# Selective scan: three quarters of x by row gathers on GpSimd, coefficients by row scatters

## The reference, cut to what matters

```
x = x + _L0_attn_a_ref(_layernorm(x, axis=-1), W_in, conv_w, conv_b, W_xproj, A_log, D_param, W_out)
x = x + _L0_ffn_ref(...)      # a mixture of 15 experts and a shared one
x = x + _L0_attn_b_ref(...)   # linear attention
...                           # experts, retention, experts, softmax attention, experts
```

## Time and profile before

| | us |
|---|---|
| median of 3 runs (lowest, highest) | 2271.25 (2269.46, 2271.72) |
| the profiled execution, its own time | 2265.08 |
| its span, first to last instruction | 2263.4 |
| busy: TensorE / VectorE / ACT / GpSimd | 1980.8 / 1702.2 / 1016.5 / 498.3 |
| mean granted clock of TensorE | 0.929 |

### The profile page before, as it was taken

One profiled execution on the slowest core, in us unless ns is written; L12 is line 12 of the kernel. 1 busy time (PEld: TensorE's weight loads), 2 busy tenths in 40 slices (PEclk: granted clock), 3 DMA queues, 4 the chain that ended last, 5 costly groups with the idle time before them and its releaser, 6 DMA issues. The chain is left out here.

```text
span 2263.4 us, 35922 instructions
## 1 busy us (share of the span) xinstructions
PE 1980.8 (88%) x12434; PEld 1484.5 (66%) x12434; DVE 1702.2 (75%) x5243; ACT 1016.5 (45%) x1596; POOL 498.3 (22%) x560
## 2 busy tenths in 40 slices
PE   5786799987999867754699978999999999979999
PEld 3554699976999823322699965566556555549998
DVE  6997788865888769999588876766766766628887
ACT  3442244433444333322344444566665665554443
POOL 1110100012000023221100014534533544230000
PEclk8998899998999987776799989999999999989999
DMA  3000100000000000000000000000000000000000
GB/s 97 6 5 4 54 1 1 1 1 1 1 1 2 13 27 1 0 1 0 1 1 1 1 1 1 1 1 1 1 1 1 1 1 1 1 1 6 11 11 15
DMA packets 17638, 15.75 MB, mean 7 GB/s; under 512 B 4209, under 2 KB 16177, under 8 KB 16946
## 3 DMA queue, kind: packets, MB, share of 16 engines
q1 hardware_dynamic: 15152, 12.66, 1.8%
q10 hardware_dynamic: 2306, 0.78, 0.2%
HBM read 10.55 MB, written 2.88 MB: 6 GB/s over the span
## 5 line engine op out<-in xcount | busy, mean ns | idle before, releaser
L2256 DVE TENSOR_REDUCE soft_mx<-psum 128x1 f32<-128x512 f32 (+3 forms) x608 | 380.4, 659 | 198.5 <-PE psum L2127 111.9
L2173 ACT ACTIVATE soft_prob<-psum 128x1024 f32<-128x1024 f32 (+3 forms) x384 | 305.1, 813 | 209.8 <-PE psum L2054 208.9
L2123 PE MATMUL psum<-soft_own,soft_stack 128*128 128x512 f32 (+3 forms) x768 | 250.4, 376 | 18.9 <-DVE soft_mx L2256 16.5
L2054 PE MATMUL psum<-soft_stack,soft_own 128*128 128x512 f32 (+3 forms) x768 | 228.4, 381 | 2.9 <-POOL soft_stack L2029 2.2
L2054 PEld LDWEIGHTS psum<-soft_stack,soft_own 128*128 128x128 f32 x768 | 121.2, 189 | 134.1 <-issue 74.7
L2123 PEld LDWEIGHTS psum<-soft_own,soft_stack 128*128 128x128 f32 x768 | 139.2, 191 | 77.7 <-DVE soft_mx L2256 63.1
L2071 PE MATMUL psum<-soft_prob,soft_v_pad 128*32 128x512 f32 (+3 forms) x1536 | 163.9, 498 | 3.5 <-ACT soft_prob L2173 2.1
L1056 DVE SCALAR_TENSOR_TENSOR x<-psum,ffn1b_cw,x 128x128 f32<-128x128 f32 x512 | 144.0, 343 | 30.1 <-PE psum L934 21.3
L1056 DVE SCALAR_TENSOR_TENSOR x<-psum,ffn0b_cw,x 128x128 f32<-128x128 f32 x512 | 144.1, 343 | 29.9 <-PE psum L934 21.5
L1056 DVE SCALAR_TENSOR_TENSOR x<-psum,ffn1a_cw,x 128x128 f32<-128x128 f32 x512 | 144.1, 344 | 29.8 <-PE psum L934 21.0
L1056 DVE SCALAR_TENSOR_TENSOR x<-psum,ffn0a_cw,x 128x128 f32<-128x128 f32 x512 | 144.1, 344 | 29.5 <-PE psum L934 21.0
(11 more groups left out here) (435 smaller groups left out, 3845.4 us busy)
## 6 DMA issues: line engine op xcount, KB each, us to landing
s_ffn_w<-in_ffn_w SPq DMA_DIRECT2D x4, 1024.0 KB, 8.3
out_x<-x SPq DMA_DIRECT2D x8, 256.0 KB, 2.3
x<-in_x SPq DMA_DIRECT2D x4, 384.0 KB, 7.4
mamba_coef_dram<-mamba_out_coef SPq DMA_DIRECT2D x8, 96.0 KB, 1.6
s_ret_w<-in_ret_w SPq DMA_DIRECT2D x1, 640.0 KB, 3.5
x<-in_x SPq DMA_DIRECT2D x4, 128.0 KB, 3.9
s_ret_cos<-in_ret_cos SPq DMA_DIRECT2D x1, 512.0 KB, 4.9
s_ret_sin<-in_ret_sin SPq DMA_DIRECT2D x1, 512.0 KB, 5.5
```

The costliest lines, as they stand in the source:

```text
L2054: ins = pe.matmul(e_ps[:, n % 2, j, low(n):BLK], own[:, u % 3, 2 * pair + j, kt * P:(kt + 1) * P], stack[:, u % HT, qb * BLK + low(n):(qb ...
L2123: ins = pe.matmul(per_head[:, n, :], stack[:, u % HT, i * P:(i + 1) * P], own[:, u % 3, g, half * BLK:half * BLK + width], start=(n == 0), ...
L2173: nc.scalar.activation(prob[:, done % PROBS, :, low(n):BLK], e_ps[:, n % 2, :, low(n):BLK], ACT.Exp, scale=float(HD) ** -0.5).then_inc(exp ...
L2256: nc.vector.tensor_reduce(mx[:, i, half, heads.start:heads.stop], bank[:, 0:width * len(heads)].rearrange("p (g k) -> p g k", k=width), AX ...
```

## The change

Three quarters of x (token tiles 2 to 7 of each batch row) are no longer loaded by four DMAs of SP, but by 24 indirect DMAs of GpSimd, 128 rows each, the row numbers taken from a new constant table `rows` of 128 x 32 integers (column n holds the rows of tile n). The table is one more load in `weights_rest`. GpSimd issues the gathers behind its first two `invert`s and a wait for `weights_rest`, ahead of its first tile. The stores of `out_coef` go from SP to GpSimd as indirect DMAs that scatter 128 rows with a column of the same table; GpSimd instead of SP waits at the end for all eight.

```
@@ shape_constants
+            "rows": np.arange(TILES * P, dtype=np.int32).reshape(TILES, P).T,
@@ mamba_scan, block.sync
-            for copies, loaded in (x_first, x_rest, later):
+            for copies, loaded in (x_first, later):
                 for dst, src in copies:
                     sp.dma_start(dst, src).then_inc(loaded, 16)
-            for tt in range(TPB):
-                sp.wait_ge(out_coef_ready, tt + 1)
-                sp.dma_start(coef_dram[slice(tt * P, (tt + 1) * P), :], out_coef[:, :, :, :]).then_inc(coef_stored, 16)
-            sp.wait_ge(coef_stored, 16 * TPB)
@@ block.gpsimd, scan
                 nc.gpsimd.tensor_copy(out_coef[:, 2, :, :], cc[:, :, 0:NS]).then_inc(out_coef_ready, 1)
+                pool.wait_ge(out_coef_ready, tt + 1)
+                pool.indirect_dma_start(coef_dram[:, :], bass.IndirectOffsetOnAxis(const["rows"][:, tt:tt + 1], 0),
+                                        out_coef[:, :, :, :].rearrange("p k b s -> p (k b s)"), None)\
+                    .then_inc(coef_stored, 16)
                 if more == 2:
                     norm.invert(pool, tt + 2)
@@ block.gpsimd
             norm.invert(pool, 0)
             norm.invert(pool, 1)
+            pool.wait_ge(*all_of(*weights_rest))
+            dst, src, loaded = x_rest
+            for a in range(2, TPB):
+                for b in range(BATCH):
+                    n = b * TPB + a
+                    pool.indirect_dma_start(dst[:, n, :], None, src,
+                                            bass.IndirectOffsetOnAxis(const["rows"][:, n:n + 1], 0))\
+                        .then_inc(loaded, 16)
             tiles(scan)
+            pool.wait_ge(coef_stored, 16 * TPB)
@@ block.vector
-            dve.wait_ge(*all_of(*x_rest))
+            dve.wait_ge(x_rest[2], 16 * BATCH * (TPB - 2))
@@ hybrid_kernel
-        x_rest = [(homes[:, b, 2:TPB, :], tokens[:, b, 2:TPB, :]) for b in range(BATCH)]
+        x_rest = x, arrays["x"].rearrange("b t c -> (b t) c")
-        loads = ((x_first, load_x_first), (x_rest, load_x_rest), (weights_first, load_first),
+        loads = ((x_first, load_x_first), (*x_rest, load_x_rest), (weights_first, load_first),
```

## The result

The median went from 2271.36 us (four runs; the first three of them gave the 2271.25 above) to 2291.75 us (four runs, 2290.36 to 2293.00): ratio 1.0093, 95% interval 1.0081 to 1.0105, which is 20.4 us slower. The forecast was 2294. The profiled execution took 2290.36 us, 25.3 more than the one of before.

A forecast was written before the change was run, and what follows sets the result against it. VectorE paces the scan; its wait for x before the first tile decides. 14.6 + 29.8 + 3.0 + 2.2 = 49.6 us against 28.60 gives 21.0, plus 2.0 for the clock: 23.0 us, median 2294 us, range 2279 to 2315.

The forecast's parts named there:

- scatters hidden: In each tile, a 1.24 us scatter on GpSimd fits its idle time: counted 0, 4.6 us kept for the range.
- Price of a gather: On GpSimd ahead of the first tile: 1.24 us per gather, 29.8 us for 24, bounds 7.9 and 52.8.
- Start: Gathers begin once `weights_rest` has landed: 10.6 + 4.0 = 14.6 us, not before 13.22, at the latest 20.4.
- Stalls by VectorE: VectorE's convolutions and SiLU product hold up GpSimd's gathers in the head: 3 us, bounds 0 and 5.9.
- Landing: The last gather lands 2.2 us after it is issued, bounds 1.6 and 5.2.
- Clock: TensorE's longer pause starts the first tile at the low clock: 2.0 us on VectorE's path, bounds 0 and 4.
- Tiles behind: From VectorE's first step inputs to the stage's end: distance unchanged but for about 2 us.
- Hidden: Rival: gathers done by 28.60 us, at most 0.52 us each, time stays at 2271 us; chance 0.09.
- half hidden: Rival: gathers on GpSimd cost 0.52 to 0.9 us each; at 0.75 us, time 2280 us; chance 0.07.
- One at a time: Rival: each gather waits for the one before to land, 2.2 us each, time 2317 us; chance 0.12.
- Starved: Rival: GpSimd gets no descriptor out during VectorE's dense stretch up to 23.63 us, time 2300 us; chance 0.10.

The follow-up runs named there:

- the kernel with the order alone: Kernel before the change, with SP issuing the later weights ahead of the rest of x and no GpSimd DMA: 2272.93 us, ratio 1.0020.
- the direct DMAs: Changed kernel with the 24 pieces of x loaded by plain DMAs of GpSimd instead of gathers: 2274.53 us, ratio 1.0024 against the kernel before.

## Why the prediction was right, point by point

The mechanism held: VectorE's one wait for all of x, ended by a DMA near 50 us (forecast 49.6, measured 49.75), everything behind it moved by the whole delay, scatters hidden. But the sum agrees better than its terms, and that is luck.

- **Price of a gather**, 1.24 us: measured 1.25. The number was right by luck, the reason wrong. I took it from GpSimd's rows as the time to work through 128 partitions; with 64 rows it is 1.21, and a plain DMA of 128 rows takes 0.56. It is a price per indirect DMA.
- **Start**, 14.6 us: measured 17.79. This step failed: I wrote that a little could come or go with the first weights, and counted nothing. SP's later weights moved up beside them and `a_log` landed 3.7 us later, so that the second `invert` ended at 16.96 us (15.95 + 1.01) instead of 13.22. The last of `weights_rest`, issued by 11.35 us and not 10.6, then released the gathers 6.4 us after that, not 4.0. The bound of 20.4 us held it.
- **Stalls by VectorE**, 3 us of at most 5.9: measured 0.8 (48.27 - 17.79, less 24 x 1.25 and plus the last gap of 0.30). Only three gathers are longer (1.13, 1.19, 1.27), while others lie wholly beside the convolution and take 0.95 (the one at 23.23 us beside VectorE's L543 from 22.60 to 24.93). The rule that I weighed, from the Trainium skill's "SBUF — State Buffer", section "Who interferes with whom", was the better guide. The trace agrees: a gather, which reads one column of row numbers, is hardly held up, a GpSimd copy is held up (0.78 against 0.24 us), and the 1.61 us above show the same the other way round.
- **Landing**, 2.2 us from the end of issuing: measured 1.48 (49.75 - 48.27).
- **Clock**, 2.0 us in the first tile: measured 0.0 (23.87 and 23.88). I compared the first tile with the last, but the first tile of the kernel before begins at the low level too, with 0.50 between 36 and 40 us and 1.00 behind it. The changed kernel does the same after its longer pause, 0.50 from 53 to 57 us and 1.00 from 61 us on, and the two groups cost in its first tile what they cost before:

```profile
63.47 1.12 PE L412 MATMUL psum<-mamba_ct,mamba_bt 128*128 128x512 f32 x2 [0.96 <-DVE mamba_bounds L634]
64.52 4.59 PE L416 MATMUL psum<-mamba_xtok,mamba_wk 128*32 128x256 f32 x32
```

- **Tiles behind**, counted at nothing: 1.85 us. The kernel without scatters has 1.96. Tiles at 1.00 take the same in both (22.25 and 22.26). Of the full tiles 1 to 5, those at 0.92 or 0.93 take 22.65 to 23.16 us before and 22.77 to 23.19 after, and there are three of them in either; the last two tiles make up most of the difference (0.46 and 0.79 us). The gathers need not be the cause: the kernel with the order alone, whose scan is that of the kernel before and starts only 3.3 us later, takes 185.37 us for the stretch (31.87 to 217.24), 3.67 more than before. So this stretch can differ by more than 1.85 us with no DMA of GpSimd in either kernel.

Too early a start (3.2 us short) and too dear stalls, landing and clock (2.2, 0.7 and 2.0 too much) cancelled, with 1.85 us behind. Against the medians, the 23.0 us that were forecast stand beside 20.4, whose interval (18.4 to 23.8 us) holds them.

*Rivals.* Hidden and half hidden: the direct DMAs show what they would have looked like, 0.56 us apiece. One at a time: no, gathers start every 1.25 us and land 2.4 us after. Starved: no, the gathers start at 17.79 us while VectorE is busy up to 27.4 us (26.12 + 1.28), and lose 0.8 us in all.

## What to carry to other kernels

Price a row gather per instruction, not per row: here 1.25 us of GpSimd for 128 rows, against 0.33 us on SP for a plain DMA of 128 rows, and look at which single wait stands behind the whole series; one wait per piece gave 17 us of the 20 back here (step inputs at 32.46 instead of 49.75 us). When a load is taken off a queue, ask what moves up into its place: 2 MB of weights that moved up beside small, urgent loads made these 3 to 4 us later. And check each term of a sum after the fact, not only the sum.

## What the runs showed of the hardware that was not expected

A gather's price on GpSimd hardly depends on its rows (1.21 us for 64, 1.25 for 128). An 8 KB load landed after 3.5, 5.2, 6.3, 8.5 or 8.9 us, depending on what went out on the other queue beside it; with the same weights cut into runs of 512 B, which went out more slowly, it was 6.3 and not 8.5. A VectorE instruction with two SBUF inputs took 1.61 instead of 0.75 us beside a GpSimd copy that started with it.
